# A sorting loop cut into 75 groups, type one-hots on ScalarE, pad rows written by SyncE

## What is computed

```python
h = jnp.maximum(_layernorm(x, axis=-1), 0.0)
W = jnp.einsum('rb,bio->rio', a, V)                      # 20 types from 8 basis matrices
seg = dst * R + etypes
agg = jax.ops.segment_sum(x[src], seg, num_segments=N * R)
h = jnp.einsum('nri,rio->no', agg.reshape(N, R, -1), W) + x @ w_loop + bias
...
x = x + relational(h)          # then three more layers that use src and dst
```

## Time and profile before

| | |
|---|---|
| median of 3 runs | 3374.0 us (3370.48 to 3389.06) |
| profiled execution, its own time | 3367.41 us |
| its span, first to last instruction | 3365.6 us |
| mean granted clock of PE | 0.848 of full speed |
| DVE busy | 2962.6 us (88%) |
| PE busy | 2794.5 us (83%) |
| POOL busy | 2157.1 us (64%) |
| ACT busy | 599.0 us (18%) |
| sorting loop, first burst to last scatter issued | 79.73 to 815.50 us |
| first instruction of the next stage | 827.49 us |

### The profile page before, as it was taken

One profiled execution on the slowest core, in us unless ns is written; L12 is line 12 of the kernel. 1 busy time (PEld: TensorE's weight loads), 2 busy tenths in 40 slices (PEclk: granted clock), 3 DMA queues, 4 the chain that ended last, 5 costly groups with the idle time before them and its releaser, 6 DMA issues. The chain is left out here.

```text
span 3365.6 us, 58070 instructions
## 1 busy us (share of the span) xinstructions
PE 2794.5 (83%) x19402; PEld 1821.4 (54%) x19402; DVE 2962.6 (88%) x8489; ACT 599.0 (18%) x1500; POOL 2157.1 (64%) x2102
## 2 busy tenths in 40 slices
PE   8888888884688999969997899999999776777752
PEld 5555555553457777746665566666666433333321
DVE  9999999995949999979999788888888489999987
ACT  3010110000420000001110111111111133333320
POOL 4777777775007777757774777767775277777740
PEclk6889899986557888869998899999999788888875
DMA  4111111111322111121111111111111011111120
GB/s 173 32 34 36 34 34 35 34 34 44 114 88 43 24 24 25 17 27 30 28 30 20 39 30 30 31 30 30 31 30 19 13 27 28 27 27 27 27 16 5
DMA packets 140073, 120.20 MB, mean 36 GB/s; under 512 B 61230, under 2 KB 123650, under 8 KB 139666
## 3 DMA queue, kind: packets, MB, share of 16 engines
q0 software_dynamic: 65952, 45.62, 8.8%
q1 hardware_dynamic: 70242, 62.69, 7.2%
q10 hardware_dynamic: 3600, 8.19, 0.6%
HBM read 85.00 MB, written 31.35 MB: 35 GB/s over the span
## 5 line engine op out<-in xcount | busy, mean ns | idle before, releaser
L1684 POOL DMA_INDIRECT flow_x<-node_table,src_indices x440 | 518.1, 1177 | 246.3 <-PE p_x_turned L1800 105.1
L731 PE MATMUL p_in_picked<-block_table 128*96 128x512 bf16 x1725 | 450.9, 425 | 95.2 <-DVE block_table L608 95.2
L608 DVE TENSOR_SCALAR block_table<-in_sources,node_numbers 128x512 bf16<-128x512 f16 x1725 | 522.8, 372 | 0.1
L1824 PE MATMUL flow_acc_bwd<-flow_onehot_j,flow_by_q 128*128 128x512 bf16 x2640 | 517.2, 328 | 0.0
L2051 POOL DMA_INDIRECT att_kv_rows<-kv_table,att_index x440 | 426.1, 968 | 139.6 <-issue 131.4
L1132 POOL DMA_INDIRECT rel_rows<-message_table,message_indices x320 | 322.9, 1009 | 298.3 <-POOLq L1349 201.1
L430 POOL DMA_INDIRECT sorted_edges<-block_table,sorted_row x416 | 402.0, 966 | 126.8 <-issue 126.2
L731 PEld LDWEIGHTS p_in_picked<-block_table 128*96 128x96 bf16 x1725 | 231.3, 138 | 288.8 <-DVE block_table L608 94.8
L1425 POOL DMA_INDIRECT sum_rows<-node_table,src_indices x280 | 270.4, 966 | 111.2 <-issue 85.0
L2087 DVE TENSOR_REDUCE att_tile_max<-p_att_scores 128x4 f32<-128x512 f32 x440 | 283.2, 684 | 24.8 <-PE p_att_scores L2201 20.5
L1460 DVE TENSOR_SCALAR sum_source_onehot<-sum_sources,node_numbers 128x512 bf16<-128x512 f16 x1000 | 300.6, 367 | 0.0
(11 more groups left out here) (349 smaller groups left out, 4909.7 us busy)
## 6 DMA issues: line engine op xcount, KB each, us to landing
flow_dst_lanes<-dst_rows SPq DMA_DIRECT2D x110, 128.0 KB, 3.0
rel_rows<-sorted_edges SPq DMA_DIRECT2D x20, 572.0 KB, 3.7
in_sources<-source_rows_in SPq DMA_DIRECT2D x69, 128.0 KB
message_table<-message_rows ACTq DMA_DIRECT2D x25, 320.0 KB, 2.2
message_table<-message_rows SPq DMA_DIRECT2D x25, 320.0 KB, 2.2
flow_x<-node_table,src_indices POOLq DMA_INDIRECT x440, 2.6
att_kv_rows<-kv_table,att_index POOLq DMA_INDIRECT x440, 2.4
sorted_edges<-block_table,sorted_row POOLq DMA_INDIRECT x416, 2.2
```

The lines of the kernel that those rows point to most:

```text
L608: last = dve.tensor_scalar(which[g % 2][:, c, :], srcs[b][:], s["node"][:, c:c + 1], None, ALU.is_equal)
L731: last = pe.matmul(pp[g % 2][0:3 * F, 0:CW], hs[:, c].rearrange("p k f -> p (k f)"), which[g % 2][:, c, :], start=(c == 0), stop=(c == NB ...
L1684: pool.indirect_dma_start(out=X[b][:, t, 0:F], out_offset=None, in_=d["nodes"], in_offset=bass.IndirectOffsetOnAxis(ap=s["idx_src"][:, g * ...
L1824: last = pe.matmul(accB[:, lo:hi], S[b][:, t, k, :], J[b][:, t, lo:hi], start=False, stop=True, skip_group_check=True)
```

## The change

The loop has CN = 75 groups and no rest. Each has four picked columns and one or two gathered ones (`GATHERED`, 116 columns in all instead of 140). The type one-hot moves from DVE to ACT, where it is two activations: the square of type minus lane, then max(1 - square, 0); the one of the next group is made behind a group's fill. The pads are written by SP: it loads the tile numbers into registers, five at a time, and issues one plain DMA per block, ahead of the first source and type loads.

```diff
@@ -41,11 +41,12 @@
...
 AHEAD, BESIDE = 8, 7
-CN = EC // CG
-CTAIL = EC - CN * CG
+CN = 75
+GATHERED = [(g + 1) * (EC - CN * CP) // CN - g * (EC - CN * CP) // CN for g in range(CN)]
+FIRST = [CP * g + sum(GATHERED[0:g]) for g in range(CN)]
 CW = CP * P
-PADS = 4
-assert CP + CTAIL <= CG and (T - EC) % PADS == 0
+PADS, PAD_REGS = 4, 5
+assert FIRST[-1] + CP + GATHERED[-1] == EC and CP + max(GATHERED) <= CG and (T - EC) % PADS == 0
 QJ = (N + 3) // 4
...
@@ -306,11 +307,17 @@
...
         def columns(g):
-            return (range(CP, CP + CTAIL), CN * CG) if g == CN else (range(CG), g * CG)
+            return range(CP + GATHERED[g]), FIRST[g]
+
+        def gathers_until(g):
+            return 16 * sum(GATHERED[g % SLOTS:g + 1:SLOTS])
+
+        def sent_before(g):
+            return 16 * sum(CP + n for n in GATHERED[g % SLOTS:g:SLOTS])
 
...
             if g >= SLOTS:
-                eng.wait_ge(sent[g % SLOTS], 16 * CG * (g // SLOTS))
+                eng.wait_ge(sent[g % SLOTS], sent_before(g))
 
...
@@ -347,17 +354,27 @@
...
                     sp.dma_start(d[n][full * P:EC, :], turned_rows[i][0:EC - full * P, full, :]).then_inc(rows_out, 16)
+                lanes_rows = d["sorted"][0:T * P, :].rearrange("(p t) w -> p t w", p=P)
+                sp.wait_ge(pads, 16)
+                sp.wait_ge(pad_ready, 1)
+                regs = [sp.alloc_register(f"last_tile_of_block{b}") for b in range(PAD_REGS)]
+                for lo in range(0, NB, PAD_REGS):
+                    n = min(PAD_REGS, NB - lo)
+                    sp.load(regs[0:n], last_of_block[:, lo:lo + n])
+                    for i in range(n):
+                        tile = sp.snap(regs[i], min_val=0, max_val=T - 1)
+                        sp.dma_start(lanes_rows[:, bass.ds(tile, 1), :], pad[:, 0:1, :]).then_inc(pads, 16)
                 sp.wait_ge(rows_out, 64)
...
                         sp.wait_ge(kinds_ready, g - RINGS + 1)
-                    at = g * CG * P
+                    at = FIRST[g] * P
                     for n, x, m in (("src_in", srcs, P), ("type_in", typs, R)):
...
                                      .to_broadcast([m, CW])).then_inc(row_in[b], 16)
-                sp.wait_ge(pads, 16)
+                sp.wait_ge(pads, 16 * (NB + 1))
 
...
@@ -378,9 +395,9 @@
...
                           allow_small_or_imprecise_dtypes=True).then_inc(consts, 1)
-                pool.iota(first_row[:], pattern=[[1, 1]], base=0, channel_multiplier=T,
+                pool.memset(negmid[:], float(-MIDDLE)).then_inc(consts, 1)
+                pool.iota(neglane[:], pattern=[[1, 1]], base=0, channel_multiplier=-1,
                           allow_small_or_imprecise_dtypes=True).then_inc(consts, 1)
-                pool.memset(negmid[:], float(-MIDDLE)).then_inc(consts, 1)
                 pool.wait_ge(recs, 1)
...
@@ -395,13 +412,6 @@
...
 
-                pool.wait_ge(recs, 2)
-                pool.wait_ge(pad_ready, 1)
-                pool.wait_ge(pads, 16)
-                for b in range(NB):
-                    pool.indirect_dma_start(
-                        out=d["sorted"], out_offset=bass.IndirectOffsetOnAxis(ap=last_row[:, b:b + 1], axis=0),
-                        in_=pad[:, 0, :], in_offset=None).then_inc(s["padded"], 16)
                 for b in range(2):
...
@@ -422,9 +432,8 @@
...
                     pool.wait_ge(filled, g + 1)
-                    if g < CN:
-                        pool.wait_ge(msg_ready, g + 1)
-                    pool.wait_ge(gathered[b], 16 * (CG - CP) * (g // SLOTS + 1))
+                    pool.wait_ge(msg_ready, g + 1)
+                    pool.wait_ge(gathered[b], gathers_until(g))
                     for j in js:
...
@@ -434,13 +443,13 @@
...
                 pool.wait_ge(row_ready, 1)
-                pool.wait_ge(s["padded"], 16 * NB)
-                for g in range(CN + 1):
-                    if g + AHEAD <= CN:
+                pool.wait_ge(pads, 16 * (NB + 1))
+                for g in range(CN):
+                    if g + AHEAD < CN:
                         gather(g + AHEAD)
...
                 for b in range(SLOTS):
-                    pool.wait_ge(sent[b], 16 * sum(len(columns(g)[0]) for g in range(b, CN + 1, SLOTS)))
+                    pool.wait_ge(sent[b], sent_before(CN + (b - CN) % SLOTS))
 
...
@@ -496,6 +505,18 @@
...
 
+                def types(g):
+                    act.wait_ge(row_in[g % RINGS], 32 * (g // RINGS) + 32)
+                    if g >= 2:
+                        act.wait_ge(coef_done, g - 1)
+                    if g >= 1:
+                        act.wait_ge(kinds_ready, g)
+                    act.activation(apart[:], typs[g % RINGS][:], ACT.Square, bias=neglane[:, 0:1]).then_inc(apart_ready, 1)
+                    act.wait_ge(apart_ready, g + 1)
+                    act.activation(kinds[g % 2][:], apart[:], ACT.Relu, scale=-1.0, bias=s["ones"][0:R, 0:1])\
+                        .then_inc(kinds_ready, 1)
+
+                types(0)
                 for g in range(CN):
...
@@ -506,7 +527,8 @@
...
                     fill(g)
-                fill(CN)
+                    if g + 1 < CN:
+                        types(g + 1)
 
...
@@ -554,8 +576,7 @@
...
                 dve.tensor_tensor(off[:], off[:], run[:, 0:NB], ALU.subtract).then_inc(cols, 1)
-                w.done(dve.tensor_scalar(cnt[:], upto[:], -1.0, 0.0, ALU.add, ALU.max))
-                dve.tensor_scalar(last_row[:], cnt[:], first_row[:, 0:1], None, ALU.add).then_inc(pad_ready, 1)
+                dve.tensor_scalar(last_of_block[:], upto[0:1, :], -1.0, 0.0, ALU.add, ALU.max).then_inc(pad_ready, 1)
                 dve.tensor_tensor(s["sq"][:], s["xc"][:], top(s["xc"][:]), ALU.subtract).then_inc(steps, 1)
...
@@ -609,12 +630,6 @@
...
 
-                def types(g):
-                    if g >= 2:
-                        dve.wait_ge(coef_done, g - 1)
-                    dve.tensor_scalar(kinds[g % 2][:], typs[g % RINGS][:], s["lane"][0:R, 0:1], None, ALU.is_equal)\
-                        .then_inc(kinds_ready, 1)
-
                 def weigh(g):
...
@@ -641,7 +656,6 @@
...
                         weigh(g - 2)
-                    types(g)
                     if g >= 3:
```

More of the change, by code:

```diff
@@ L178, in build @@
                          for name in ("sort", "rel1", "rel2", "sum", "flow", "att")}
-        s["padded"] = ctx.enter_context(nc.semaphore("block_pads_moved"))
         with ExitStack() as with_records:
@@ L251, in sort_edges @@
         coef = [spare(1, [P, CP, NBASIS]) for _ in range(2)]
+        apart = spare(1, [R, CW])
         blk = s["begin"][:, 0:EC]
@@ L265, in sort_edges @@
         extra = sb(st, "extra_row", [P, 1])
-        first_row = sb(st, "first_row_of_lane", [P, 1])
-        last_row = sb(st, "last_row_of_block", [P, NB], U32)
+        last_of_block = sb(st, "last_tile_of_block", [1, NB], I32)
         negmid = sb(st, "minus_middle", [P, 1])
+        neglane = sb(st, "minus_lane", [R, 1])
         pad = sb(st, "pad_rows", [P, PADS, ROW])
@@ L291, in sort_edges @@
          got, v_ready, which_ready, kinds_ready, pick_done, pick_taken, coef_done, coef_taken, z_done, z_taken,
-         msg_ready, filled, steps, row_ready, index_ready, w_in, w_made, w_taken, pad_ready) = (sem(st, f"sort_{n}") for n in (
+         msg_ready, filled, steps, row_ready, index_ready, w_in, w_made, w_taken, pad_ready, apart_ready) = (sem(st, f"sort_{n}") for n in (
              "padding_set", "dst_loaded", "edges_loaded", "attr_loaded", "consts", "pads_written", "vector_steps", "column_ready",
@@ L298, in sort_edges @@
              "slots_filled", "steps", "row_ready", "index_ready", "weights_in", "weights_made", "weights_taken",
-             "pad_ready"))
+             "pad_ready", "types_apart"))
         row_in = [sem(st, f"sort_rows_in{b}") for b in range(RINGS)]
```

## The result

The changed kernel takes 3394.9 us (median of 17 runs, 3389.37 to 3400.31), the kernel before 3374.0 (17 runs beside them, 3365.56 to 3389.06): a ratio of 1.0062, 95% interval 1.0052 to 1.0072. It is slower, by 20.9 us; the forecast was 3404. The profiled execution took 3398.83 us (span 3397.0) at a granted clock of 0.85, as before.

What follows compares the result with a forecast made beforehand. DVE and POOL were taken as both full in the sorting stage. With 75 groups DVE sets the end: 71 x 9.92 us plus a 32.6 us tail ends 29.6 us later, so 3374 + 29.6 = 3404 us, range 3370 to 3448.

Steps and rivals of the forecast that it cites:

- The groups: Sorting loop: 75 groups in place of 69 give DVE six more full bursts, weightings and reductions, which nothing hides.
- The period: One group on DVE in the sorting loop: 7.53 + 1.26 + 1.13 = 9.92 us.
- stretch: Excess of a DVE burst over 6.63 us, its length while POOL stands still; 0.97 us kept, each 0.1 worth 7.1.
- The gain of the types: Type one-hot leaving DVE saves 0.26 us a group; ACT's two activations cost nothing, priced up to 0.58 us each.
- The pads: SP before the first burst: pad writes at 0.33 us cost nothing; rival at 1.26 us delays it 9 us (chance 0.05).
- POOL is relieved: POOL loses 25 pad DMAs and 24 gathers (30 us), starts gathers earlier and could end at 758, before 815.50.
- One sign of being right: In most groups of the sorting loop, POOL has idle time that DVE's reduction ends.
- Starvation: Rival: POOL DMAs held for whole DVE bursts, 6.4 us each; one burst in four gives 3438 us; chance 0.15.
- 13 held bursts: Whole-burst holds of 6.4 us each that POOL could take before it ends last in the sorting stage: (845 - 758)/6.4.
- The tail: From the last burst's start to the last scatter's issue: 17.7 + 1.0 + 11 x 1.264 = 32.6 us.
- The sum: Sorting stage's last DMA issued at 845.1, 29.6 us later than 815.50; 3374 + 29.6 = 3404 us.
- the median of the runs is 6.6 above it: Offset from the kernel before's profiled execution, 3367.4 us, to its run median, added to reach the forecast.

Runs made afterwards that it cites:

- pads_only: The kernel before with the pads written by SP alone (69 groups, types on DVE): 3358.34 us, ratio 0.9973 to the kernel before.
- types_only: The kernel before with the type one-hots on ACT alone (69 groups, pads on POOL): 3356.42 us, ratio 0.9959 to the kernel before.
- groups_only: The kernel before with the 75 groups alone (types on DVE, pads on POOL): 3404.31 us, ratio 1.0103 to the kernel before.

## Why the prediction was right

*The groups.* Six more full bursts, with nothing to hide them, were the reason for the loss, and they are: 69 to 75 groups costs 1.03% alone and 1.05% with the other two edits made.

*The period.* 9.92 us was said, 9.905 measured. Its parts were 1.26 and 1.13 us (measured 1.25 and 1.13) and a stretch of 0.97, measured 0.92. Six bursts of about 6.64 us with a held DMA beside them are in that mean; without them it is 1.00. The reason given for keeping 0.97, that five or six DMAs still fall into a burst, holds: from group 4 on 5.3 DMAs end in a burst on average, where it was 6.0. But their number doesn't fix the stretch, as the last section shows, and the three other kernels with 75 groups and 25 one-hots on DVE had 0.73, 0.79 and 0.83. That 0.97 came out within 0.05 is in part luck.

*The gain of the types.* 0.26 us a group was said; the two pairs of kernels gave 0.175 and 0.19 us of period. The runs show why that is less: without the type one-hot the stretch grows (0.83 to 0.92, 0.73 to 0.79), in part because fewer DMAs are held. ACT's two instructions cost 0.72 us each, above the upper end of 0.58, and nothing came of it: in the stretch 300 to 400 us PE's matmuls waited for DVE's burst alone (9.5 us).

*The pads.* SP's five register loads took 0.73 to 1.52 us instead of 2.09, the writes 0.33, the lower end. The row of instructions by line shows min, median and max in ns and the first and last start:

```profile
L363 SPq TENSOR_LOAD <-last_tile_of_block x5: 733/1330/1516, 44.5 to 60.8; - x5
```

```profile
L366 SPq DMA_DIRECT2D sorted_edges<-pad_rows x25: 332/332/552, 45.4 to 63.9; - x25
```

The first source load went out at 64.33 (63 was said) and the first burst began at 79.53, no later than before. This rival fell.

*POOL is relieved.* It could end at 758, the prediction said. The last scatter at 842.59, less the 42.8 us that pauses took above the usual 0.30 and 35.1 us of held DMAs, gives 764.7; the other 6.7 us are DMAs of a little over 1.264 us. One sign of being right did not come: POOL's idle time ended behind DVE's reduction in 26 of the 75 groups, not in most; nearly as much of its spare time went into held DMAs as into pauses.

*Starvation.* This rival came true in small: in the loop about every eleventh group holds one DMA for the length of the burst, six times, beside the first gather. In DVE's and POOL's timelines one of them is:

```profile
336.37 6.64 DVE L629 TENSOR_SCALAR block_table<-in_sources,node_numbers 128x512 bf16<-128x512 f16 x25
```

```profile
337.26 5.88 POOL L439 DMA_INDIRECT sorted_edges<-block_table,sorted_row  x1 [1.27 <-issue]
343.44 0.97 POOL L439 DMA_INDIRECT sorted_edges<-block_table,sorted_row  x1 [0.30 <-issue]
```

The DMA ends when the burst does (343.14 and 343.01), and the burst is as short as the one of the earlier trace rows that ran alone. The Trainium skill ("SBUF — State Buffer", section "Who interferes with whom") has an exclusive lock under which one engine waits fully for the whole instruction of the other. The seven held DMAs look like it, but POOL stands there through the rest of a burst of 25 instructions (5.88 us) and not through one; the bursts at 7.6 us, with DMAs of 0.96 us inside, do not look like it.

The loss stayed under the 13 held bursts that POOL could afford, so the end didn't move, and the timelines show why it stayed small. From group 4 on the twelve kernels have 32 held DMAs. Each is the first that POOL issues into a burst that began between two DMAs, and 31 of them ended a pause of about 1 us or more (the other is the one shown for pads_only). None of the 488 bursts that began beside a running DMA held one. So in these runs nearly every held DMA stands behind a pause, where POOL was ahead of DVE and had time to lose.

*The tail.* 32.6 us from the last burst to the last scatter were said, 31.84 measured: the last reduction but one ends 17.18 us after that burst's start (17.7 was said), and POOL starts 0.77 us behind it, not 0.97.

*The sum.* The stage ended 27.1 us later instead of 29.6. The profiled executions differ by 31.4, the rest of the program being 4.3 us longer in this one (2554.4 against 2550.1 after the last scatter; over the twelve profiled executions it runs from 2546.0 to 2554.9, so no cause need be sought in the change). The term that was mis-sized is the last: "the median of the runs is 6.6 above it". That offset belonged to one execution of the kernel before. The changed kernel's profiled execution lies 3.9 us above its median, so the two offsets shift the difference by 10.5 us, from 31.4 to the 20.9 of the medians. With the 2.5 and 4.3 us that accounts for the 9 us between 3404 and 3394.9. The chance of a loss over 0.5% was put at 0.74; the loss is just above that bound, and the interval with it.

## What to carry to other kernels

Two engines that share work and slow each other have a crossing: count what each needs per group (here 1.264 us per DMA on POOL, 6.56 + 1.25 + 1.13 = 8.94 us plus the stretch on DVE) and put the split there; this change walked past it, and 70 groups instead of 75 made the same code faster than before. When both are full, the next gain is work moved to a third engine with idle time (two of 25 one-hots on ACT: 1.3% at 75 groups, 0.7% at 72), and the split is then set anew.

## What the runs showed that was not expected

A busy share of nearly 100% on DVE didn't mean that DVE was the limit. With 69 groups its bursts grew from 7.60 to 7.89 us when 0.26 us of other work was taken away, so that the period kept POOL's 10.2 us, and DVE still showed 99.65 of 100 us busy: the time went into the instructions. With POOL at leisure the stretch was 0.73 to 0.97, with POOL full and DVE ahead 1.23 to 1.25.

Single one-hots show where it goes in. In the burst of the earlier trace rows their median is 0.33 us; the one below took 0.56, and POOL's DMA ended while it ran, at 305.49 (timeline of the kernel before):

```profile
304.53 0.96 POOL L416 DMA_INDIRECT block_table<-message_table,message_index_in  x1 [0.31 <-issue]
305.04 0.56 DVE L608 TENSOR_SCALAR block_table<-in_sources,node_numbers 128x512 bf16<-128x512 f16 x1
```

In the bursts from group 4 on, in all twelve kernels, every one-hot over 0.42 us was running when a DMA of POOL ended. A burst has 5.0 of these before, 4.6 in the changed kernel and 6.0 in types_only, at stretches of 0.97, 0.92 and 1.25, so each is worth about 0.2 us. In types_only 388 of the 389 DMAs that end in a burst lengthen a one-hot so far, in groups_only only 3.6 of 5.0 in a burst. What decides it for a single DMA, and which DMA behind a pause is held, the runs don't settle.

A POOL DMA that is first after a pause can take 1.11 or 1.12 us instead of 0.96 (307.13), and POOL's pauses for DVE are shown as "issue".
